# Loading heads 2 and 3 before the QKV stage ends, with fill matmuls in attention's first three slots

## What is computed

```
q, k, v = einsum(normed input, qkv_w[0..2]);  q, k = rope(q), rope(k)
scores = einsum('bqhd,bkhd->bhqk', q, k) / sqrt(HD)
scores = where(tril, scores, -1e30)
p = softmax(scores, axis=-1)
o = einsum('bhqk,bkhd->bqhd', p, v)
```

## Time and profile before

| | us |
|---|---|
| median of 3 executions | 2325.4 (2321.68 to 2331.71) |
| profiled execution | 2319.34 |
| its span | 2317.6 |
| QKV and the change-over, to slot 2's first scores | to 337.16 |
| mean granted clock of TensorE | 0.974 |

### The profile page before, as it was taken

One profiled execution on the slowest core, in us unless ns is written; L12 is line 12 of the kernel. 1 busy time (PEld: TensorE's weight loads), 2 busy tenths in 40 slices (PEclk: granted clock), 3 DMA queues, 4 the chain that ended last, 5 costly groups with the idle time before them and its releaser, 6 DMA issues.

```text
span 2317.6 us, 34022 instructions
## 1 busy us (share of the span) xinstructions
PE 2189.7 (94%) x11560; PEld 1796.4 (78%) x11560; DVE 1324.6 (57%) x1734; ACT 1066.4 (46%) x1596; POOL 997.2 (43%) x621
## 2 busy tenths in 40 slices
PE   6989889999988998899999999998799999999999
PEld 4777766666657887788788989996678888888887
DVE  6787756777747987333333277676464364364222
ACT  2444538888876877412312356655322122122111
POOL 0111138999987777000000478774153253153110
PEclk9999979999998998999999999999899999999999
DMA  5687763333335665445544478877565565465443
GB/s 182 215 247 244 236 174 88 106 96 98 99 89 195 241 217 204 155 139 170 167 147 159 173 274 300 306 283 288 190 205 176 156 200 174 162 207 174 153 137 100
DMA packets 208916, 424.60 MB, mean 183 GB/s; under 512 B 16482, under 2 KB 132194, under 8 KB 181940
## 3 DMA queue, kind: packets, MB, share of 16 engines
q1 hardware_dynamic: 208820, 423.31, 55.5%
HBM read 284.31 MB, written 138.67 MB: 183 GB/s over the span
## 4 chain that ended last, share of the span: by engine, by line
PE 67%; DMA 11%; DVE 9%; ACT 5%; issue 4%; POOL 2%; SPq 2%; DVEq 0%; ACTq 0%; POOLq 0%
PE s_psF L2691 7%; PE s_psF L2692 7%; PE s_psF L2693 7%; PE s_m_psG L2317 7%; PE s_m_psU L2317 7%; PE s_w_psA L1901 5%; PE s_w_psB L1901 5%; PE s_psO L922 4%; PE s_psS L868 4%; DMA s_q_xc<-xP 4%; DMA s_f_q<-wq 3%; PE s_psX L899 3%; DMA y<-s_f_xb 2%; DVE s_a_mx L948 1%; PE s_w_psT L1933 1%
## 5 line engine op out<-in xcount | busy, mean ns | idle before, releaser
L2691 PE MATMUL s_psF<-s_f_wh,s_f_xh 128*128 128x512 f32 x1024 | 401.3, 392 | 12.2 <-DVE s_f_xl L2570 7.5
L2693 PE MATMUL s_psF<-s_f_wh,s_f_xl 128*128 128x512 f32 x1024 | 399.6, 390 | 0.0
L1053 POOL TENSOR_TENSOR s_a_pl<-s_a_pf,s_a_ph 128x1024 fp32r<-128x1024 f32 x128 | 301.9, 2392 | 22.2 <-ACT s_a_pf L1010 22.0
L2566 ACT ACTIVATE s_f_xh<-s_f_xl 128x2048 fp32r<-128x2048 f32 x64 | 122.7, 1917 | 380.9 <-PE s_psF L2693 309.5
L2664 POOL TENSOR_TENSOR s_f_xb<-s_f_xb,s_f_fb 128x512 f32<-128x512 f32 x64 | 97.1, 1516 | 358.2 <-DMA s_f_xb<-x 339.9
L2691 PEld LDWEIGHTS s_psF<-s_f_wh,s_f_xh 128*128 128x128 f32 x1024 | 193.2, 189 | 55.8 <-DVE s_f_xl L2570 10.3
L948 DVE TENSOR_REDUCE s_a_mx<-s_psS 128x1 f32<-128x512 f32 (+2 forms) x248 | 179.3, 754 | 99.0 <-PE s_psS L876 98.6
L2069 POOL TENSOR_TENSOR s_w_yl<-s_w_y,s_w_yh 128x1024 fp32r<-128x1024 f32 x32 | 76.1, 2400 | 369.4 <-ACT s_w_yh L1981 369.4
L2693 PEld LDWEIGHTS s_psF<-s_f_wh,s_f_xl 128*128 128x128 f32 x1024 | 193.0, 188 | 40.3
L2570 DVE TENSOR_TENSOR s_f_xl<-s_f_xl,s_f_xh 128x2048 fp32r<-128x2048 f32 x64 | 160.7, 2511 | 81.2 <-ACT s_f_xh L2566 81.2
L2692 PE MATMUL s_psF<-s_f_wl,s_f_xh 128*128 128x512 f32 x512 | 200.5, 392 | 0.0
(11 more groups left out here) (316 smaller groups left out, 5674.7 us busy)
## 6 DMA issues: line engine op xcount, KB each, us to landing
s_f_xl<-xnT SPq DMA_DIRECT2D x64, 1024.0 KB, 5.7
s_q_xt<-xT SPq DMA_DIRECT2D x16, 1024.0 KB, 7.7
s_q_xc<-xP SPq DMA_DIRECT2D x16, 1024.0 KB, 9.8
hsD<-s_q_hs SPq DMA_DIRECT2D x16, 1024.0 KB, 4.9
s_w_hin<-hsD SPq DMA_DIRECT2D x16, 1024.0 KB, 4.8
hs<-s_w_res SPq DMA_DIRECT2D x16, 1024.0 KB, 3.9
s_m_raw<-giT SPq DMA_DIRECT2D x32, 512.0 KB, 4.6
mlpT<-s_m_mo SPq DMA_DIRECT2D x64, 256.0 KB, 2.4
```

The lines of the kernel that those rows point to most:

```text
L1053: pool.tensor_tensor(pl[:, r, cols], pf[:, j - 1], ph[:, r, cols], ALU.subtract).then_inc(pl_ok, 1)
L2691: pe.matmul(out[:], xh[:, u % 2, kt], high(c, kt), start=(kt == 0), stop=False)
L2693: mm = pe.matmul(out[:], xl[u % 3][:, kt], high(c, kt), start=False, stop=(kt == KD - 1))
```

## The change

Four edits. (1) The loads of heads 2 and 3 are issued behind QKV's drain slot 2, and attention's slots 0 to 3 no longer load. (2) In that hook attention's part is called ahead of `prepare_sync`, so the order there is: stores of tile 14, loads of heads 2 and 3, the waits and six transfers of `prepare_sync`, stores of tile 15. (3) In slots 0, 1 and 2 two matmuls of 96 x 128 by 96 x 512 stand behind each group of scores; their result, in `psX[0]` in slots 0 and 1 and in the second bank of `psO` in slot 2, is never read and is overwritten by the next work in that bank. (4) GpSimd waits in slot 2, ahead of its first remainder, for all of QKV's stores, since the remainders lie where the stores' sources lay.

```
             if i == 1:
                 ...
                 load(sp, Step(None, 1, HEADS), 1)
+            if i == 2:
+                load(sp, Step(None, 2, HEADS), 2)
+                load(sp, Step(None, 3, HEADS), 3)
...
-                if live(0):
+                if live(0) and not (s.reg is None and s.off < RING):
                     load(sp, s, p)
...
+            def keep_busy(s, p):
+                bank = psX[0][:, 0:512] if s.off < 2 else psO[:, 1]
+                for _ in range(2):
+                    pe.matmul(bank, ka[0:K3, p, 0:P], ka[0:K3, p, 0:512], start=True, stop=True)
...
                 for i in range(SG):
                     if live(0):
                         scores(s, slot, i)
+                    if s.reg is None and s.off < 3:
+                        keep_busy(s, slot)
...
                 for j in range(1, PK):
+                    if j == 1 and s.reg is None and s.off == 2:
+                        qkv["stored"](pool, TILES)
...
             def ahead(i):
+                att["sync_ahead"](sp, i)
                 w1["prepare_sync"](sp, i)
-                att["sync_ahead"](sp, i)
```

## The result

| | before | changed |
|---|---|---|
| median, 17 executions each | 2326.3 us (2318.4 to 2333.5) | 2340.7 us (2329.7 to 2344.7) |
| ratio | 1 | 1.0052, 95% interval 1.0036 to 1.0067 |
| median, second time, 35 and 12 executions | 2330.1 us | 2334.7 us |
| ratio, second time | 1 | 1.0028, 1.0005 to 1.0052 |
| profiled execution, span | 2319.3, 2317.6 | 2342.3, 2340.6 |

The changed kernel is slower. By the ratios it is 12.1 us of 2326 in the first comparison and 6.5 of 2330 in the second; the medians alone differ by 14.4 and 4.6. The forecast was 8.1 us slower, 2333.5, with a range up to 2339. The first ratio on the 2325.4 that the forecast started from gives 2337.5; the first median itself, 2340.7, lies 1.7 us above the range. The step's mechanism shows in the trace almost as written; the two terms of the sum were off by +0.8 and -1.3 us.

The account below looks back on a forecast made before the run. The chain of waits through TensorE was taken to bound the kernel; slot 2 starting 4.5 us later plus 3.6 us of fill there gave +8.1 us, 2333.5 on the 2325.4 median, range 2318 to 2339.

Parts of the forecast that it names:

- What bounds: Start of slot 2: VectorE's maxima lie below the key rows' wait, so head 2's transfer costs 1.48 us, not 2.74.
- The loads, +4.5: Loads ahead of the write stage's weights on SP's queue delay ScalarE, then VectorE; slot 2 starts 4.5 us later.
- the lateness of line 1022: ScalarE's first half of head 0's turned maxima, behind weights landing 5.5 to 6.4 us later; 6.0 taken.
- What else moved: Turned maxima's transfer, tile 15's stores, GpSimd's preparation (ends 343.5, remainder near 349) and new wait: later, but covered, no cost.
- The fill, +3.6 in slot 2: Fill at 1.2 GHz in slot 2 costs 4.3 us, less waits of 0.56 and 0.15; free in slots 0 and 1.
- No clock by the fill in slot 2: Fill shaped like the scores does not restore the clock in slot 2; it returns 4.9 us into slot 3.
- The sum, +8.1: Whole kernel: 4.5 us from slot 2's later start plus 3.6 from its fill, nothing taken back from slot 3 on.
- B: Rival: the clock comes back in slot 2 by about its second group; +2.6 us, 2328; chance 0.20.
- C: Rival: weights late by at most 1.7 us, fill keeps the clock through slot 2; -6.5 us, 2319; chance 0.14.
- D: Rival: the clock does not come back in slot 3; +15.6 us, 2341; chance 0.08.

Follow-up runs that it names:

- e4: Changed kernel with the six write-stage transfers ahead of the loads of heads 2 and 3 again, and without the fill; ratio 0.9994 (0.9972 to 1.0016).
- e8: Changed kernel profiled once more with no further edit; 6.5 us over before, ratio 1.0028 (1.0005 to 1.0052).
- e10: Changed kernel with head 3's load moved behind the six transfers, head 2's still ahead; executed once, slot 3 at 33.3 us behind head 0's first scores.
- e5: Changed kernel, but in slot 1 VectorE makes the low half of head 0's turned maxima behind its last three groups of maxima; ratio 1.0007 (0.9985 to 1.0029).
- e2: Kernel before with the fill alone, loads not moved; ratio 1.0012 (0.9984 to 1.0039).
- e3: Changed kernel with the six write-stage transfers ahead of the loads of heads 2 and 3 again, fill kept; ratio 1.0013 (0.9991 to 1.0035).
- e6: Changed kernel with the six transfers ahead of the loads again and fill in slots 0 and 1 alone; ratio 0.9982 (0.9962 to 1.0002).
- e11: Repeat of e6, same kernel once more for its time; ratio 0.9988 (0.9966 to 1.0010).
- e9: Changed kernel with six fill matmuls instead of two behind each group of slot 2; executed once, slot 2 lasted 24.0 us.
- e12: As e9, but slot 2's six fills take 128 rows of bf16 constants instead of 96 rows of keys; executed once, slot 2 lasted 14.1 us.

## Why the prediction was right, and where it was off

- **What bounds: right.** Slot 2 could not start before VectorE's maxima, so the wait for key rows was worth 1.5 us and not 2.74. e4 has slot 2 at 14.5 against 15.7, 1.2 less.
- **The loads, +4.5: right in mechanism, mis-sized.** Measured +5.3 (20.98 - 15.71), and +5.5 in the second pair. The term of the sum that was short is the lateness of line 1022: 6.0 taken, 6.8 measured. The weights landed 6.6 us later, and 0.17 more went into ScalarE's wait for the small transfers. Both limits of the prediction come close to that. The issue was 6.3 us later and not 5.5, because the first three DMAs of head 2 took 2.06 us behind tile 14's stores and not 1.28. The bytes, 1.57 MB at 243 GB/s, are 6.5 us (the prediction has 6.4 and then took 6.0). Two further traces speak for the bytes: in e8 the weights were issued 0.9 us later than in the changed kernel's first profile, 7.7 us behind head 0's scores, and landed at the same 13.3; in e10 they were issued 4.4 us later than before and landed only 2.8 us later, near the 3.2 of one load's bytes. These are the issue and ScalarE's conversion in e8, and the issue in e10:

```profile
328.73 0.35 SPq L1163 DMA_DIRECT2D s_w_raw<-wo  x1
...
334.34 1.26 ACT L1177 ACTIVATE s_w_wh<-s_w_raw 128x1264 fp32r<-128x1264 f32 x1 [6.25 <-DMA s_w_raw<-wo]
```

```profile
328.59 0.35 SPq L1167 DMA_DIRECT2D s_w_raw<-wo  x1
```

  The rest of the chain was sized right: from line 1022 to slot 2 the prediction has 4.2 us and the trace 4.26. All of it passed through VectorE's order (e5), from 1.5 to 1.9 us of lateness on, counted from the first profile of before.
- **What else moved: right.** The turned maxima were issued at 342.47 and nobody waited for them; GpSimd's preparation ended at 347.7 and its first remainder began at 354.73, 22.6 and 29.7 us behind head 0's scores; the prediction's 343.5 and 349 are 22.1 and 27.6 on that clock, so the cover was larger. The new wait cost nothing that shows (e4 has it).
- **The fill, +3.6 in slot 2: mis-sized.** Measured +2.3 (15.54 against 13.27; e2 has 15.57, and e3 against e6 and e11 gives 2.5). Counting two waits for VectorE of 0.56 and 0.15 was too few. Slot 2 of the kernel before has more of them: in each of the last three groups TensorE's next scores start within 0.15 us of the end of VectorE's reduction, as these two timelines of the kernel before show (VectorE, then TensorE, whose 350.43 stands in the earlier trace rows). They carry no idle time, because the modelled ends of the matmuls ahead of them reach over the gap (the masks ahead of 345.23 stand at 344.95 with 0.44 us, to 345.39). By the starts of the matmuls the five waits can still be measured: from the start of the last matmul of a group to the next scores' start, less the 0.13, 0.09 or 0.07 us that the same step takes in the changed kernel, they are 0.86, 0.39, 0.09, 0.22 and 0.35 us, 1.9 in all. That leaves 2.4 of the fill's 4.3 us, and 2.3 were measured. The fill in slots 0 and 1 cost nothing, as predicted.

```profile
344.22 0.96 DVE L948 TENSOR_REDUCE s_a_mx<-s_psS 128x1 f32<-128x768 f32 x1 [0.45 <-PE s_psS L876]
346.52 1.09 DVE L948 TENSOR_REDUCE s_a_mx<-s_psS 128x1 f32<-128x896 f32 x1 [1.34 <-PE s_psS L876]
349.05 1.23 DVE L948 TENSOR_REDUCE s_a_mx<-s_psS 128x1 f32<-128x1024 f32 x1 [1.45 <-PE s_psS L876]
```

```profile
345.23 1.12 PE L868 MATMUL s_psS<-s_a_k,s_a_q 96*128 96x512 f32 x2
...
347.66 1.22 PE L868 MATMUL s_psS<-s_a_k,s_a_q 96*128 96x512 f32 x2
```

- **No clock by the fill in slot 2: right,** in seven profiles with the 96-row fill there, and e9 is the strongest of them. The reason that I gave, that the fill is of the same shape and operands as the scores, fits e12 as far as one run goes: with a fill of another shape the clock came back. The Trainium skill ("TensorE: Matmul & The Clock Gate", Part 1) ties the release to sustained activity; e9's rows show 20 us of it at 0.50, so the busy time in the profile does not tell by itself when the clock returns.
- **The sum, +8.1.** At slot 3 the two pairs of profiles have +7.5 and +7.8 and at head 31 +7.4 on the mean of both. The two errors, +0.8 and -1.3, cancel in part, and that the sum came so near is luck to that extent.
- **On the whole kernel:** +12.1 us (8.4 to 15.6) and +6.5 (1.2 to 12.1). The 7.4 of the trace lies in the second interval and 1 us under the first. The kernel before measured against itself gave 1.0010 (0.9988 to 1.0031). Whether the first comparison holds a further cost of a few us elsewhere stays open. Behind the MLP's first matmul the two profiles of before took 1380.1 and 1377.1 us and the two of the changed kernel 1381.1 and 1384.9; no edit touches that part, and the ten variants range from 1376.6 to 1383.0, so I take it for scatter, but two profiles each cannot show it.
- **The rivals.** B and C did not happen. C's gain is not there either when its condition is met (e4 and e3: -0.4 and +1.2 us at head 31 for the -6.5 that it was priced at), because it rested on a clock that stays up through slot 2. D did not happen: in all profiles but e12 the clock came back 2.9 to 6.2 us into slot 3.

## What to carry to other kernels

Moving a load up in a DMA queue moves down everything behind it; price each of those by who waits for it in order, here a weight that nobody needs for 350 us but which stood in ScalarE's stream ahead of the one small result that VectorE, and so TensorE, needed next. A short dose-response (both loads, one, none ahead) settles such a question with one trace each, where a ratio of whole times with an interval 0.3% wide or wider can't. And fill matmuls pay only if they change the clock in the stretch where it is low: look there first, and at what kind of matmul brought it back in the trace at hand.

## What the runs showed of the hardware that I had not expected

With matmuls mostly of 96 and 98 rows TensorE stayed at the lower clock through a slot of 24.0 us in which it was busy without a gap (e9); with six bf16 matmuls of 128 rows behind the first group of scores it was back at 2.4 GHz by the next group (e12). What it was in the six that mattered is open. The form of this that looks best was not run: weights first, and a few fills of 128 rows in slot 2 alone.

Three DMA issues of the same kind took 2.05 to 2.49 us on SyncE in the ten profiles where a head's load follows directly on a tile's four stores (1 MB in 512-byte rows), and 1.28 for the next load of the changed kernel. The stores are not the only case: in attention of the kernel before three of them took 2.60 us at 351.78 with no store just ahead. What slows an issue, no run here separates.
